# A selective scan on Trainium2: summing both units of a batch over the states in products of 128 columns

## What is computed

```
xz = xn @ W_in;  xi, z = split(xz)                 # 256 channels each
u = silu(conv(xi));  dt_r, Bm, Cm = split(u @ W_xproj)
delta = softplus(dt_r @ W_dt + b_dt);  A = -exp(A_log)   # A: 256 channels x 64 states
h = h * exp(delta_t * A) + (delta_t * u_t) * B_t   # for each of the 128 tokens
y_t = sum over the 64 states of h * C_t
out = ((y + u * D) * silu(z)) @ W_out
```

## Time and profile before

| | us |
|---|---|
| median of 3 runs (range) | 1403.27 (1398.83 to 1403.92) |
| profiled execution, own time | 1392.82 |
| its span | 1390.8 |
| PE / PEld / DVE / ACT / POOL busy | 1114.5 / 800.1 / 850.9 / 529.5 / 570.0 |
| mean granted clock | 0.848 |

### The profile page before, as it was taken

The page is one execution under the profiler, slowest core; times in us unless marked ns, Lnnn a source line. Parts: engine busy times, 40 slices in busy tenths (PEclk is TensorE's granted clock), DMA queues, the critical chain, the costliest instruction groups (busy, mean ns, idle before and its releaser), DMA issues. The chain is left out here.

```text
span 1390.8 us, 29830 instructions
## 1 busy us (share of the span) xinstructions
PE 1114.5 (80%) x12054; PEld 800.1 (58%) x12065; DVE 850.9 (61%) x1500; ACT 529.5 (38%) x1322; POOL 570.0 (41%) x382
## 2 busy tenths in 40 slices
PE   5568898898887898999547598689476899866895
PEld 2158787887875454545336255545366454543695
DVE  6577888888884476366713476567512676755233
ACT  2433434434431363255114164156133565612121
POOL 4169988989864702210157310020434201000432
PEclk9656988888878599999869799699688998987998
DMA  2099687778855200000075100000365000000793
GB/s 105 0 207 216 196 214 206 203 208 211 204 168 198 65 1 1 0 1 2 1 201 182 33 2 1 1 1 1 116 199 185 1 2 1 1 1 23 259 302 99
DMA packets 74232, 139.75 MB, mean 100 GB/s; under 512 B 8129, under 2 KB 28369, under 8 KB 73745
## 3 DMA queue, kind: packets, MB, share of 16 engines
q1 hardware_dynamic: 70128, 129.67, 32.8%
q0 software_dynamic: 3968, 8.18, 1.6%
HBM read 128.06 MB, written 14.82 MB: 103 GB/s over the span
## 5 line engine op out<-in xcount | busy, mean ns | idle before, releaser
L658 ACT ACTIVATE shifted_a<-scores,nmax_a 128x128 f32<-128x128 f32 x768 | 208.5, 387 | 85.7 <-DVE nmax_a L624 85.7
L1125 PE MATMUL decay<-delta,A_pairs 32*128 32x127 f32 x2048 | 178.6, 335 | 49.2 <-DVE small_pack L1219 18.9
L1200 ACT ACTIVATE decay<-decay 128x1016 f32<-128x1016 f32 x128 | 128.7, 1010 | 197.8 <-PE decay L1125 197.8
L1125 PEld LDWEIGHTS decay<-delta,A_pairs 32*128 32x128 f32 x2048 | 155.5, 235 | 69.6 <-DVE small_pack L1219 23.6
L624 DVE TENSOR_REDUCE nmax_a<-scores 128x4 f32<-128x512 f32 x192 | 123.6, 686 | 108.3 <-PE scores L563 105.9
L361 POOL TENSOR_TENSOR rstd<-ve,neghalf 128x4 f32<-128x4 f32 x30 | 31.5, 1051 | 281.7 <-DVE ve L347 281.7
L630 DVE COPY PTs_a<-PT 128x512 f32<-128x512 f32 x192 | 123.6, 681 | 4.6 <-PE PT L571 4.6
L571 PE MATMUL PT<-mamba_pack,shifted_a 128*128 128x128 f32 x768 | 114.1, 293 | 4.3 <-DVE PTs_a L630 2.7
L1460 POOL DMA_INDIRECT results<-xs_s x76 | 73.0, 960 | 104.2 <-DVE xs_s L1632 96.6
L571 PEld LDWEIGHTS PT<-mamba_pack,shifted_a 128*128 128x128 f32 x768 | 88.5, 149 | 36.8 <-issue 20.1
L247 PE MATMUL norm_ps<-identb 128*128 128x512 bf16 x180 | 59.6, 446 | 52.2 <-DVE ve L347 51.5
(11 more groups left out here) (395 smaller groups left out, 2238.3 us busy)
## 6 DMA issues: line engine op xcount, KB each, us to landing
pos_bias<-du_rows SPq DMA_DIRECT2D x72, 256.0 KB, 4.9
small_pack<-L3f_w SPq DMA_DIRECT2D x15, 768.0 KB, 5.0
XN<-du_rows SPq DMA_DIRECT2D x38, 256.0 KB, 5.1
XNT<-du_rows SPq DMA_DIRECT2D x38, 256.0 KB, 4.8
O<-du_rows SPq DMA_DIRECT2D x36, 256.0 KB, 4.9
masked_cos<-du_rows SPq DMA_DIRECT2D x36, 256.0 KB, 4.9
masked_sin<-du_rows SPq DMA_DIRECT2D x36, 256.0 KB, 4.8
small_pack<-L2f_w SPq DMA_DIRECT2D x15, 514.0 KB, 5.0
```

The costliest lines, as they stand in the source:

```text
L658: t = nc.scalar.activation(shifted[u % 4][:, j, :], scores[u % 4][:, j, :], ACT.Exp, scale=-1.0, bias=nmax[:, u % 4, j:j + 1])
L1125: t = nc.tensor.matmul(decay[k % DEEP][:, s, i, 1:S], A_pairs[strip, c, 4 * q + i, :, :].rearrange("p j n -> p (j n)"), delta[strip, c, b ...
L1200: nc.scalar.activation(x, x, ACT.Exp).then_inc(decayed, 1)
```

## The change

- The states have one space of three areas (AREA = 8192 values each), unit n in area n % 3. Unit n waits for the batch of unit n - 3.
- Both units of a batch are summed at once: one product per token has the 64 columns of each unit, 128 in all, so there are 1024 gather products of 128 columns for 2048 of 64. A batch's gather is cut into seven parts, in the slots of tiles 2 to 8 after the batch's last tile; both units are turned back two slots after it. The next batch's C is placed after that gather.
- The output is written into u. The inputs' work space, du and A lie in the same space, B2 and C2 in the areas of CT and CTOK.
- small_pack, row_pack, rel, the q and k masks, the causal masks and run_on are allocated where the states lay, after the scan. So their loads, CT's and CTOK's are issued in the output block: rel, the first 1957 columns of small_pack, CT, row_pack, CTOK, the other 7093 columns of small_pack, then the store of the table; SP waits for the last four at the end of the block.
- The memsets of q_mask and k_mask move from VectorE at the start to GpSimd in the output block; ScalarE waits for them.

```diff
+AREA = 8 * B * S
...
+    def allocate_above(self):
+
+        sb = self.sb_above
+        self.small_pack = sb("small_pack", [128, SMALL_N])
+        self.row_pack, self.rel = sb("row_pack", [128, ROWS_N]), sb("rel", [128, 2, D])
+        self.q_mask, self.k_mask = sb("q_mask", [128, T], BF16), sb("k_mask", [128, T], BF16)
+        self.causalb, self.strictb = sb("causalb", [S, S], BF16), sb("strictb", [S, S], BF16)
+        self.flipb = sb("flipb", [S, S], BF16)
+        self.run_on = sb("run_on", [128, 17 * 16])
...
-            sp.dma_start(m.row_pack[:], d["rows"].to_broadcast([128, ROWS_N])).then_inc(m.loaded_rest, 16)
-            sp.dma_start(m.CT[:], d["ctx_feat"]).then_inc(m.loaded_rest, 16)
-            sp.dma_start(m.CTOK[:], d["ctx_tok"]).then_inc(m.loaded_rest, 16)
-            sp.dma_start(m.rel[:], d["rel_pos"]).then_inc(m.loaded_rest, 16)
...
-            m.dve_steps.inc(nc.vector.memset(m.q_mask[:], 0.0))
-            m.dve_steps.done(dve, nc.vector.memset(m.k_mask[:], 0.0))
-            nc.vector.memset(m.q_mask[32:33, :], 1.0)
-            nc.vector.memset(m.k_mask[32:33, :], BIG)
...
+            sp.wait_ge(m.loaded_rest, 16)
+            sp.dma_start(m.rel[:], m.dram["rel_pos"]).then_inc(m.loaded_rest, 16)
+            first = SMALL_AT["L0f_router"][0]
+            sp.dma_start(m.small_pack[:, 0:first], m.dram["small"][:, 0:first]).then_inc(m.loaded_small, 16)
+            sp.dma_start(m.CT[:], m.dram["ctx_feat"]).then_inc(m.loaded_late, 16)
+            sp.dma_start(m.row_pack[:], m.dram["rows"].to_broadcast([128, ROWS_N])).then_inc(m.loaded_late, 16)
+            sp.dma_start(m.CTOK[:], m.dram["ctx_tok"]).then_inc(m.loaded_late, 16)
+            sp.dma_start(m.small_pack[:, first:], m.dram["small"][:, first:]).then_inc(m.loaded_late, 16)
             sp.wait_ge(copied, 1)
             sp.dma_start(tab, tableT[:]).then_inc(stored, 16)
             sp.wait_ge(stored, 16)
...
+            sp.wait_ge(m.loaded_late, 64)
 
         @block.vector
         def _(dve):
-            dve.wait_ge(m.loaded_rest, 80)
+            dve.wait_ge(m.loaded_rest, 32)
...
-            act.wait_ge(m.loaded_rest, 80)
+            act.wait_ge(m.loaded_rest, 16)
             nc.scalar.activation(mask, m.mask8[:], ACT.Copy).then_inc(widened, 1)
 
             act.wait_ge(widened, 1)
+            act.wait_ge(masks_set, 2)
             nc.scalar.activation(m.q_mask[0:1, :], mask[0:1, :], ACT.Copy)
             nc.scalar.activation(m.k_mask[0:1, :], mask[0:1, :], ACT.Copy, scale=-BIG)
...
+            for at in (m.q_mask, m.k_mask):
+                m.pool_steps.inc(nc.gpsimd.memset(at[:], 0.0))
             nc.gpsimd.memset(m.onesb[:], 1.0)
             m.pool_steps.done(pool, nc.gpsimd.memset(m.run_on[:], 1.0))
-            nc.gpsimd.memset(m.run_on[:, 0:16 * 16].rearrange("p (e g) -> p e g", g=16)[:, :, 0], 0.0)
+            m.pool_steps.done(pool, nc.gpsimd.memset(m.run_on[:, 0:16 * 16].rearrange("p (e g) -> p e g", g=16)[:, :, 0], 0.0))
+            nc.gpsimd.memset(m.q_mask[32:33, :], 1.0).then_inc(masks_set, 1)
+            pool.wait_ge(masks_set, 1)
+            nc.gpsimd.memset(m.k_mask[32:33, :], BIG).then_inc(masks_set, 1)
+            pool.wait_ge(masks_set, 2)
             pool.wait_ge(widened, 1)
             pool.wait_ge(m.loaded_small, 16)
...
-        u, gate, delta, du = (sb(name, [128, IC, T]) for name in ("u", "gate", "delta", "du"))
-        A = sb("A", [128, IC, STATE])
+        u, gate, delta = (sb(name, [128, IC, T]) for name in ("u", "gate", "delta"))
         A_pairs = sb("A_pairs", [128, IC, QUADS, 2, STATE])
         D_order = sb("D_order", [128, IC, 128])
-        B2, C2 = sb("B2", [128, T]), sb("C2", [128, T])
+        B2, C2 = m.CT, m.CTOK[:].rearrange("p b d -> p (b d)")
         Cz = sb("Cz", [128, S, 32])
         du_stored = [m.sem(f"du_stored{h}") for h in range(2)]
-        mamba_inputs(nc, m, u, gate, delta, du, A, A_pairs, D_order, B2, C2, Cz, du_stored)
-        scan_block(nc, m, u, delta, du, A_pairs, D_order, B2, C2, Cz, du_stored)
-        mamba_output(nc, m, gate, du)
-
-
-def mamba_inputs(nc, m, u, gate, delta, du, A, A_pairs, D_order, B2, C2, Cz, du_stored):
+        with ExitStack() as scan:
+            space = scan.enter_context(nc.sbuf_tensor("states", [128, 3 * AREA], F32, side="right"))
+            du = space[:, 3 * AREA - IC * T:].rearrange("p (c t) -> p c t", c=IC)
+            mamba_inputs(nc, m, u, gate, delta, du, space, A_pairs, D_order, B2, C2, Cz, du_stored)
+            scan_block(nc, m, u, delta, space, A_pairs, D_order, B2, C2, Cz, du_stored)
+        m.allocate_above()
+        mamba_output(nc, m, gate, u)
...
-        h = [m.small_pack[:, 0:S * PAIRS], sb("h1", [128, S * PAIRS])[:]]
-        at_token = [a.rearrange("p (x t) -> p x t", t=S) for a in h]
+        area = lambda n: n % 3 * AREA
+
+        def at_token(b, token):
+            first = space[:, area(IC * b) + token:area(IC * b) + token + 1]
+            return bass.AP(first.tensor, first.offset,
+                           [first.ap[0], [area(IC * b + 1) - area(IC * b), IC], [S, PAIRS]])
...
-            sp.wait_ge(summed, UNITS - 1)
-            sp.dma_start(m.small_pack[:], m.dram["small"]).then_inc(m.loaded_small, 16)
...
-            def gather(n, part):
-                b = n // IC
+            def gather(b, part):
                 if part == 0:
-                    pe.wait_ge(scanned, (n + 1) * PER)
+                    pe.wait_ge(scanned, (b + 1) * BOTH)
                     pe.wait_ge(c_placed, b + 1)
-                    if n >= 2:
-                        pe.wait_ge(sum_copied, n - 1)
-                half = part // 2
-                for turn in range(8 * (part % 2), 8 * (part % 2) + 8):
+                    if b >= 2:
+                        pe.wait_ge(sum_copied, b - 1)
+                for turn in range(32 * part // PARTS, 32 * (part + 1) // PARTS):
+                    half = turn // 16
                     for i in range(4):
-                        token = 64 * half + 16 * i + turn
-                        t = nc.tensor.matmul(Y[32 * i:32 * i + 32, n % 2, half, :], Cz[:, token, :],
-                                             at_token[n % 2][:, :, token], start=(turn == 0), stop=(turn == 15))
-                if part == 3:
+                        token = 64 * half + 16 * i + turn % 16
+                        t = nc.tensor.matmul(Y[32 * i:32 * i + 32, b % 2, half, :, :], Cz[:, token, :],
+                                             at_token(b, token), start=(turn % 16 == 0), stop=(turn % 16 == 15))
+                if part == PARTS - 1:
                     t.then_inc(summed, 1)
 
-            def turn_back(n):
-                b, c = n // IC, n % IC
-                pe.wait_ge(sum_copied, n + 1)
-                if n >= 2:
-                    pe.wait_ge(y_copied, n - 1)
-                for j in range(2):
-                    rows = slice(64 * j, 64 * j + 64)
-                    for half in range(2):
-                        at = slice(64 * half, 64 * half + 64)
-                        nc.tensor.matmul(YT[rows, n % 2, at], D_order[:, c, rows],
-                                         u[:, c, b * S + 64 * half:b * S + 64 * half + 64], start=True, stop=False)
-                        t = nc.tensor.matmul(YT[rows, n % 2, at], Ys[n % 2][:, half, :],
-                                             m.w("alternate")[:, rows], start=False, stop=True)
+            def turn_back(b):
+                pe.wait_ge(sum_copied, b + 1)
+                if b >= 1:
+                    pe.wait_ge(y_copied, b)
+                for c in range(IC):
+                    for j in range(2):
+                        rows = slice(64 * j, 64 * j + 64)
+                        for half in range(2):
+                            at = slice(64 * half, 64 * half + 64)
+                            nc.tensor.matmul(YT[rows, c, at], D_order[:, c, rows],
+                                             u[:, c, b * S + 64 * half:b * S + 64 * half + 64], start=True, stop=False)
+                            t = nc.tensor.matmul(YT[rows, c, at], Ys[:, half, c, :], m.w("alternate")[:, rows],
+                                                 start=False, stop=True)
                 t.then_inc(sum_turned, 1)
 
-            for k in range(TILES + 18):
+            for k in range(TILES + 12):
                 if k < TILES:
                     multiply(k)
-                if k >= 11 and (k - 11) % 8 < 4 and (k - 11) // 8 < UNITS:
-                    gather((k - 11) // 8, (k - 11) % 8)
-                if k >= 17 and (k - 17) % 8 == 0 and (k - 17) // 8 < UNITS:
-                    turn_back((k - 17) // 8)
+                b, slot = (k - BOTH - 2) // BOTH, (k - BOTH - 2) % BOTH
+                if 0 <= b and slot < PARTS:
+                    gather(b, slot)
+                if 0 <= b and slot == PARTS + 2:
+                    turn_back(b)
 
         @block.scalar
         def _(act):
             def place_c(b):
```

(60 more changed lines are left out.)

24 lines of the change are left out of this document (10 added, 14 removed).

## The result

The changed kernel takes 1417.25 us (1412.23 to 1427.28, 4 runs) where the kernel before takes 1401.05 (1398.79 to 1403.92, 4 runs): a ratio of 1.0099 [1.0057, 1.0141]. So it is slower by half a per cent to one, by an interval that in the second comparison just reaches 1, where I forecast 0.9% faster. Medians and ranges here count every execution; the ratios leave out executions more than 1.5% above the fastest of their kernel. The profiled execution took 1412.23 us, its span 1410.4.

The account below looks back on a forecast made before the run. No engine was free in the scan: TensorE's gather slots set the pace, with GpSimd's product second as the floor. Scan -27.5, tail +4.8 and output block +10.0 gave -12.7 us, so 1390.6 us, own range 1380 to 1398.

Parts of the forecast that it names:

- Gather: TensorE's gather in the scan: 128-column records at 36 ns high clock, 63 low; a part costs 1.3 or 2.3 us.
- floor of issue: Gather pricing: today's 30 ns per 64-column record at either clock is set by instruction issue, so wider records gain.
- -27.5 us in the scan: Scan stage: 307.3 us forecast against 334.8 now, with later batches at 38.2 us each.
- The rival on the operand's reads: Gather: scattered fp32 reads set the pace, 61 ns a record at either clock; scan 340.9, total 1428 us; 12%.
- low slot: Scan: TensorE's time for one tile at the low clock; 1.6 gather slots a batch were forecast low, 5.4 high.
- The clock: Scan: clock low when each gather begins, returning after 6.7 us, costing 1.6 low slots a batch.
- rival of a return after 10 us: Scan: clock returns later, 2.4 low slots; batch 39.7 us, scan -17, total 1401 us; 12%.
- VectorE's new wait: Scan: first tile of a batch's second unit waits for the previous batch's gather, at most 0.3 us a batch.
- The tail: Behind the last scan: whole last batch summed, 12.1 us for 8.8, plus 1.5 for turn-back and copies; +4.8 us.
- The output block: Moved loads delay the table's store and SP: next stage starts 24.2 us in instead of 14.3; +10.0 us.
- Start: Kernel start: loads and memsets moved away gain zero, at best half a microsecond.
- The sum: Whole kernel: -27.5 + 4.8 + 10.0 = -12.7 us, giving 1390.6 us.

Follow-up runs that it names:

- second comparison: The changed kernel run once more unaltered, against the kernel before: 1397.88 against 1393.58 us, 1.0058 [0.9999, 1.0116].
- contig: Changed kernel with the gather reading its columns side by side, not 512 bytes apart (wrong sums, only time read): 1372.78 us against 1393.58, 0.986.
- inter: Changed kernel with a unit's eight tiles interleaved so gather reads lie together, results kept: 1402.19 us against 1406.15 for the kernel before, ratio 0.9833.
- early: Changed kernel with each batch's gather begun one slot earlier: 1403.57 us, 1.0094 of the kernel before.
- before_twice: The kernel before, unaltered, profiled again; its second feed-forward and last stretch took 98.3 and 117.7 us.
- before_inter: The kernel before, with 64-column records, given interleaved states: 1441.74 us, 1.0242 of the kernel before.
- after: First profile of the changed kernel as built; the profiled execution took 1412.23 us.
- filled: Changed kernel with interleaved states, table store on ScalarE's queue and twelve filler products in each slot without gather: 1376.86 us, 0.9906 of the kernel before.
- filled2: Changed kernel with interleaved states, store on ScalarE's queue and fillers only behind the first gather: 1364.98 us, 0.9832 of the kernel before.

## Why the prediction was wrong

*Gather: the step that failed.* I priced a 128-column record at 36 ns high and 63 low, from an attention whose operand is contiguous, and took today's 30 ns at either clock for a floor of issue. It costs 57.5 ns at either clock. The premise was right (at the high clock the columns do not set the rate: contig takes 31 ns), the conclusion was not: the rate could be that of issue or that of the operand's reads, and I chose without a row that separates them. The runs do: 31 ns side by side, 57.5 scattered, and 15.8 for 64 columns where I had put the floor at 30. One was near: 64 columns in 30 ns and 128 contiguous ones in 36 don't fit one price a column, so either the floor or the layout differs, and the layout was in the code. The records fell by half, their price rose by 1.9: the gather's time stayed as it was, and of -27.5 us in the scan -1.8 to -4.3 came. The rival on the operand's reads, which I gave 12%, is what happened. It said 61 ns, scan 340.9, tail 15.6 us and 1428; measured were 57.5, 330.5, 14.2 and 1417. The scan came out 10 us shorter than in it, since the gathers were mostly at the high clock: 0.96 from 287.5 to 311. By the rival's own terms without a low slot a batch is 34.9 + 7 x 1.12 - 2.0 + 0.7 = 41.4 us and the scan about 330.

*The clock.* With cheap reads it was as forecast in one gather of contig, low from 239.7 to 246.5, 6.8 us; in inter it took some 14 us, longer than in my rival of a return after 10 us. With the scattered reads of the kernel as built it took 2 us, not 6.7, in the gather at 287.54.

*VectorE's new wait.* I allowed 0.3 us a batch; it is 2.47. The size follows from the record's price (the gather is late), and early showed it costs nothing of its own.

*The tail.* +4.8 forecast, +3.4 and +5.7 found, so the total came out near by luck: the terms were others. The gather takes 14.2 us for 8.8 (256 records at 55 ns, wherever the clock stands), +5.4 and not +3.3. What stands behind it takes 2.7 us, where before had 4.7, and 2.0 of those were a wait of TensorE in the turn-back of before, which I read over (timeline of before, the scan's end):

```profile
421.47 3.73 PE L1142 MATMUL Y<-h,Cz 128*32 128x64 f32 x126 [1.05 <-issue]
...
427.94 0.48 PE L1158 MATMUL YT<-mamba_pack,Ys 128*64 128x64 f32 x2 [2.03 <-issue]
```

before_twice has 1.45 us of such a wait in its tail, before_inter 4.5, after and contig none, and that is much of why the tail before reads 11.3 in one profile and 13.5 in another. With cheap reads the changed tail is 11.6 to 12.7 us, not 18.3: 2 us less in the gather, and 3.5 less behind it, the wait and the 1.5 us that I had added for the second turn-back.

*The output block.* +10.0 forecast, +7.6 and +5.6 found, about 3 us too dear. The order of events was right: store behind the loads, SyncE last. The loads landed 444.0 - 426.0 = 18 us in, not 20, and SyncE ended at 21.2 instead of 23.9. The before side moved too, 14.3 to 16.2 us between two profiles.

*Start.* Zero forecast; profiles of one kernel differ by 3 us there.

*The sum.* The measured stages give about -3 + 4.5 + 6.5 = +8 us, 0.6%, and the two comparisons say +16 and +4. With a record near the one I believed in, contig shows -29 + 0 + 7 = -22 beside before, and its median is 20.8 us below: the plan was sound but for that term.

## What to carry to other kernels

Before a wider instruction is priced from a row of the same shape, compare the operands' strides as well: an operand that used one fp32 element in 16 bytes cost this kernel twice what its columns cost side by side at the high clock, and nothing more at the low one. A rate that the array's clock doesn't move can belong to the issue or to the reads; look for a row, or make a run, that tells them apart before taking the cheaper. And a change of layout alone can move the clock: after reads are made cheap, look at the granted clock first. A new wait is a cost of its own only if the engine that ends it was not late anyway.

## What had not been expected of the hardware

- A gather record of 64 columns, four column groups in turn, takes 15.8 ns at the high clock when read side by side (before_inter, 126 records in 1.99 us). The Trainium skill says that start to start never drops below about 25 ns (TensorE: Matmul & The Clock Gate, Wait — 56ns, not 53.3ns?); the measurement differs, and decides for this shape.
- With the same instructions in the same order, the layout alone moved the mean granted clock of the scan from 0.84 to 0.53 (before and before_inter), TensorE being busier in the second.
- Products that kept TensorE busy without a gap for 51.7 us at the 1.2 GHz level did not raise it; it was up some 6 us into a gather with records of 128 columns (filled), and with the same fillers between gathers it then stayed at 1.00 over 190 us (filled2).
- Two stretches of unchanged code had two levels, 8 us apart each, that went with the chip or the hour.
